# The second attention's scores: three precision passes in the rows of one matmul per head, in place of three 480-column matmuls against a block-diagonal key tile

## The reference, cut to what matters

```python
# layer 1: query = layernorm(x), kv_source = ctx_1024 (8 sequences x 120 keys x 512)
q = (query @ w_q.T).reshape(B, T_q, 16, 32)          # 16 heads of 32 features
k = (kv_source @ w_k.T).reshape(B, T_kv, 16, 32)
v = (kv_source @ w_v.T).reshape(B, T_kv, 16, 32)
attn = softmax(einsum('bqhd,bkhd->bhqk', q, k) * 32 ** -0.5)
x = x + einsum('bhqk,bkhd->bqhd', attn, v).reshape(B, T_q, 512) @ w_o.T
```

## Time and profile before

| | |
|---|---|
| median of 3 runs | 1472.74 us (1472.26 to 1474.9) |
| the profiled execution | 1471.78 us |
| its span | 1469.7 us |
| PE busy | 1321.1 us, 90% |
| DVE busy | 852.8 us, 58% |
| ACT busy | 670.9 us, 46% |
| POOL busy | 576.5 us, 39% |

### The profile page before, as it was taken

The page is one execution under the profiler, slowest core; times in us unless marked ns, Lnnn a source line. Parts: engine busy times, 40 slices in busy tenths (PEclk is TensorE's granted clock), DMA queues, the critical chain, the costliest instruction groups (busy, mean ns, idle before and its releaser), DMA issues. The chain is left out here.

```text
span 1469.7 us, 27325 instructions
## 1 busy us (share of the span) xinstructions
PE 1321.1 (90%) x10010; PEld 797.8 (54%) x10010; DVE 852.8 (58%) x1726; ACT 670.9 (46%) x1890; POOL 576.5 (39%) x755
## 2 busy tenths in 40 slices
PE   6996666758999999999959999999999999899995
PEld 3544444436777777777634444444444444476663
DVE  5566999957888888887746655122221213354450
ACT  3332666628777777777723521111111112255552
POOL 1002688843354554545220004777700200145624
PEclk9997999989999999999979999999999999999998
DMA  6042000020011111111146103021120600268845
GB/s 232 29 172 87 1 1 2 1 87 17 9 45 59 45 52 52 45 59 59 45 143 67 29 1 87 1 59 32 27 59 0 215 1 29 94 171 188 210 57 72
DMA packets 85140, 96.99 MB, mean 66 GB/s; under 512 B 41968, under 2 KB 51344, under 8 KB 85008
## 3 DMA queue, kind: packets, MB, share of 16 engines
q1 hardware_dynamic: 67600, 73.04, 16.3%
q0 software_dynamic: 13248, 21.15, 7.7%
q10 hardware_dynamic: 4160, 1.05, 0.3%
HBM read 56.82 MB, written 38.45 MB: 65 GB/s over the span
## 5 line engine op out<-in xcount | busy, mean ns | idle before, releaser
L1406 DVE SCALAR_TENSOR_TENSOR shared_hf<-shared_ps_u,shared_sg 128x512 f32<-128x512 f32 x64 | 44.2, 691 | 275.6 <-PE shared_ps_u L105 261.2
L1133 POOL DMA_INDIRECT lists<-shared_load,shared_index x128 | 126.8, 991 | 167.6 <-DVE shared_sk L1274 126.3
L105 PE MATMUL shared_ps_g<-program_xs,program_wgu 128*128 128x512 f16 x768 | 178.7, 383 | 3.2 <-PEq L97 3.2
L896 ACT ACTIVATE attention_prob<-attention_ps_s,attention_nmax 128x120 f32<-128x120 f32 x512 | 177.2, 365 | 6.2 <-DVE attention_nmax L793 6.1
L1445 PE MATMUL shared_ps_y<-shared_wd,shared_hid 128*128 128x512 f16 x768 | 176.1, 379 | 2.0 <-DVE program_res L1432 2.0
L105 PE MATMUL shared_ps_u<-program_xs,program_wgu 128*128 128x512 f16 x768 | 176.7, 380 | 0.0
L1375 ACT ACTIVATE shared_sg<-shared_ps_g 128x512 f32<-128x512 f32 x64 | 38.2, 597 | 215.6 <-PE shared_ps_g L105 215.6
L1295 POOL DMA_INDIRECT program_x<-xn_rows,program_ex_slots x40 | 38.8, 969 | 243.6 <-PE experts_ps_x L1657 148.3
L105 PEld LDWEIGHTS shared_ps_g<-program_xs,program_wgu 128*128 128x128 f16 x768 | 75.6, 98 | 95.1 <-issue 6.1
L1445 PEld LDWEIGHTS shared_ps_y<-shared_wd,shared_hid 128*128 128x128 f16 x768 | 75.0, 98 | 92.8 <-DVE program_res L1432 2.4
L105 PEld LDWEIGHTS shared_ps_u<-program_xs,program_wgu 128*128 128x128 f16 x768 | 75.3, 98 | 91.3 <-issue 1.1
(11 more groups left out here) (276 smaller groups left out, 2565.4 us busy)
## 6 DMA issues: line engine op xcount, KB each, us to landing
xn_rows<-attention_g_xn SPq DMA_DIRECT2D x32, 256.0 KB, 2.3
xt_tiles<-attention_gT SPq DMA_DIRECT2D x32, 256.0 KB, 2.1
out_rows<-program_res SPq DMA_DIRECT2D x32, 256.0 KB, 2.1
program_xs<-xt_tiles SPq DMA_DIRECT2D x28, 256.0 KB, 5.0
program_x<-in_x SPq DMA_DIRECT2D x2, 3072.0 KB, 15.7
att_qr<-in_sh_guT SPq DMA_DIRECT2D x8, 512.0 KB, 4.1
program_x<-in_dyn_gT SPq DMA_DIRECT2D x8, 512.0 KB, 4.4
program_x<-in_dyn_uT SPq DMA_DIRECT2D x8, 512.0 KB, 5.5
```

Of the source, the lines that this page charges most:

```text
L105: last = pe.matmul(out, lhs(a, k), rhs(b, k), start=n == 0, stop=n == len(terms) - 1)
L896: last = act.activation(prob[:, c, h, :], ps_s[c % 2][:, h, :], ACT.Exp, bias=nmax[:, d % 2, c, h:h + 1], accum_out=rsum[:, d % 2, n:n + 1])
L1133: pool.indirect_dma_start(out=io["lists"], out_offset=bass.IndirectOffsetOnAxis(ap=index[:, t, k:k + 1], axis=0), in_=load[:, t, k, :], in ...
L1406: dve.scalar_tensor_tensor(hf[:, c % 2], ps_u[c % 2][:, :], HS / WS, sg[:, c % 2], ALU.mult, ALU.mult).then_inc(s["hf"], 1)
```

## The change

The scores are made by head, 16 matmuls of 120 columns for a tile in place of 12 of 480. The contraction runs over 96 rows: rows 0 to 31 hold the head's 32 features of the high queries against high keys, rows 32 to 63 high queries against low keys, rows 64 to 95 low queries against high keys. So the three passes are summed inside one matmul.

For this, a head's 32 rows of `qT` (which stand at rows 0, 32, 64 or 96) have to be moved to other rows. `spread` does that with 12 transfers inside SBUF: three parts times four row groups, each of 32 rows with four pieces of 256 bytes. They are issued by SP, per tile for the queries (`packed_queries`) and per sequence for the keys (`packed_keys`; pieces of 240 bytes). `g.queries` and `g.keys` have two buffers each; `g.queries` lies where `simb` and `rs` of the earlier stages lay. `g.kbd`, its memset and `block_keys` go.

The queries are made one step earlier (in step u-2, LEAD 6 in place of 5) and all that stands before them moves with them. `qT` has one buffer instead of two, so ACT's high part for a tile waits until the transfers of the tile before have landed (`q_in`).

```diff
+COPIES = 3 * HC
-def block_keys(pool, g, b, c):
...
+def spread(sp, to, parts, done):
+    for n, src in enumerate(parts):
+        for r in range(HC):
+            sp.dma_start(to[n * DH:(n + 1) * DH, r::HC, :], src[r * DH:(r + 1) * DH, :, :]).then_inc(done, 16)
+def packed_keys(sp, g, b):
+    cols = slice(b * J, (b + 1) * J)
+    hi, lo = g.k1[:, 0, :, cols], g.k1[:, 1, :, cols]
+    spread(sp, g.keys[:, b % 2], (hi, lo, hi), g.keys_in[b % 2])
+def packed_queries(sp, g, u, qT, done):
+    spread(sp, g.queries[:, u % 2], (qT[:, 0], qT[:, 0], qT[:, 1]), done[u % 2])
 # setup, SP
                 sp.dma_start(g.x[:, NT - 12:NT, :], xs[:, NT - 12:NT, :]).then_inc(x_in[1], 16)
+                sp.wait_ge(job_hi, last_job[3])
+                sp.wait_ge(job_lo, last_job[3])
+                packed_keys(sp, g, 0)
                 sp.wait_ge(job_mm, len(jobs))
 # setup, POOL
-                pool.memset(g.kbd[:, :, :, :, :], 0.0).then_inc(kbd_zero, 1)
...
-                    block_keys(pool, g, 0, c)
 # attention1
-    LEAD, LAG = 5, 9
+    LEAD, LAG = 6, 9
-        qT = m.sb("qT", [P, 2, 2, KC, P], f16)
+        qT = m.sb("qT", [P, 2, KC, P], f16)
 # SP, step(t, d)
                         sp.dma_start(raw[:, :], io["sh_guT"][bass.ds(b * P, P), :]).then_inc(w_in, 16)
+                        if b + 1 < B:
+                            need(sp, c4["s_mm"], KC * t)
+                            packed_keys(sp, g, b + 1)
                     u = t - 7
                     if live(u):
                         sp.wait_ge(lg.ok, u + 1)
                         sp.dma_start(io["xn_rows"]...)
+                    u = t + 2
+                    if live(u):
+                        sp.wait_ge(s["q_hi"], u + 1)
+                        sp.wait_ge(s["q_lo"], u + 1)
+                        need(sp, c4["s_mm"], KC * (u - 1))
+                        packed_queries(sp, g, u, qT, q_in)
+                    u = t - 7
+                    if live(u):
                         sp.wait_ge(s["g_lo"], u + 1)
                         sp.dma_start(io["xt_tiles"]...)
 # POOL, step(t, d)
-                    if live(t) and live(t + 1) and d == TB - 1:
-                        b = t // TB
-                        for c in range(KC):
-                            pool.wait_ge(c4["s_mm"], KC * t + c + 1)
-                            block_keys(pool, g, b + 1, c)
 # ACT, c == 3
-                        u, q = t + 1, (d + 1) % 2
+                        u = t + 2
                             act.wait_ge(s["q_mm"], u + 1)
-                            need(act, c4["s_mm"], KC * (u - 1))
-                            act.activation(qT[:, q, 0], ps_q[:, :, :], ACT.Copy, scale=SC1 / WS).then_inc(s["q_hi"], 1)
+                            need(act, q_in[(u - 1) % 2], 16 * COPIES * ((u - 1) // 2 + 1))
+                            act.activation(qT[:, 0], ps_q[:, :, :], ACT.Copy, scale=SC1 / WS).then_inc(s["q_hi"], 1)
 # PE
                 def scores(u, d, c):
+                    b = u // TB
                     if c == 0:
-                        pe.wait_ge(s["q_lo"], u + 1)
-                    if d == 0:
-                        pe.wait_ge(g.keys_ok, KC * HC * (u // TB) + HC * c + HC)
+                        pe.wait_ge(q_in[u % 2], 16 * COPIES * (u // 2 + 1))
+                    if c == 0 and d == 0:
+                        pe.wait_ge(g.keys_in[b % 2], 16 * COPIES * (b // 2 + 1))
                     need(pe, c4["exp"], KC * u + c - 1)
-                    matmuls(pe, ps_s[c % 2][:, :, :], lambda a, _: qT[:, d % 2, a, c, :], lambda a, _: g.kbd[:, a, c, :, :],
-                            ks=(0,)).then_inc(c4["s_mm"], 1)
+                    for h in range(HC):
+                        n = c * HC + h
+                        last = pe.matmul(ps_s[c % 2][:, h, :], g.queries[0:3 * DH, u % 2, n, :], g.keys[0:3 * DH, b % 2, n, :],
+                                         start=True, stop=True)
+                    last.then_inc(c4["s_mm"], 1)
 # PE, DVE, ACT, POOL: u = t + 1 becomes u = t + 2 for transposes of x, xT and the queries,
 # and apply, inverse_root and statistics go from t + 2, t + 3, t + 5 to t + 3, t + 4, t + 6
```

More of the change, by code:

```diff
@@ L699, in attention1 @@
         centred, xs_in = m.sem("centred"), m.sem("xs_in")
+        q_in = [m.sem(f"q_in{n}") for n in range(2)]
         rows_out = [m.sem(f"rows_out{n}") for n in range(2)]
@@ L756, in step @@
                 def step(t, d):
-                    u = t + 3
+                    u = t + 4
                     if live(u):
-                        ln.inverse_root(pool, g, u, (d + 3) % 4)
+                        ln.inverse_root(pool, g, u, d % 4)
                     u, q = t - 6, (d + 2) % 4
@@ L842, in step @@
                         lg.statistics(dve, g, t - 4, d, waits=False)
-                    if live(t + 2):
-                        ln.apply(dve, g, t + 2, (d + 2) % 4, s["xt_mm"])
+                    if live(t + 3):
+                        ln.apply(dve, g, t + 3, (d + 3) % 4, s["xt_mm"])
                     if live(t):
@@ L849, in step @@
                         prob_low(t - 1, 2)
-                    if live(t + 5) or live(t + 4):
-                        ln.before(dve, t + 5)
+                    if live(t + 6) or live(t + 5):
+                        ln.before(dve, t + 6)
                     u, q = t - 2, d % 2
@@ L855, in step @@
                         dve.tensor_tensor(oT[:, q, 1], ps_x[:, :, :], oT[:, q, 0], ALU.subtract).then_inc(s["o_lo"], 1)
-                    if live(t + 5) or live(t + 4):
-                        ln.statistics(dve, g, t + 5, (d + 1) % 4, waits=False)
+                    if live(t + 6) or live(t + 5):
+                        ln.statistics(dve, g, t + 6, (d + 2) % 4, waits=False)
                     if live(t):
                         maximum(t, d, 3)
-                    u, q = t + 1, (d + 1) % 2
+                    u = t + 2
                     if live(u):
                         dve.wait_ge(s["q_hi"], u + 1)
-                        dve.scalar_tensor_tensor(qT[:, q, 1], ps_q[:, :, :], SC1 / WS, qT[:, q, 0], ALU.mult,
+                        dve.scalar_tensor_tensor(qT[:, 1], ps_q[:, :, :], SC1 / WS, qT[:, 0], ALU.mult,
                                                  ALU.subtract).then_inc(s["q_lo"], 1)
@@ L921, in step @@
                             exps(t, d, c)
[L922 removed]
+                        u, q = t + 2, d % 2
                         if c == 0 and live(u):
@@ L927, in step @@
                     if isinstance(t, int) and t == NT + 1:
-                        act.wait_ge(g.keys_ok, B * KC * HC)
+                        for n in range(2):
+                            act.wait_ge(g.keys_in[n], 16 * COPIES * B // 2)
                         tokens(act, g, io, 0, 0, xs_in)
@@ L1007, in step @@
                         outputs(t - 2, 3)
-                    u = t + 1
+                    u = t + 2
                     if live(u):
@@ L1039, in step @@
                         need(pe, s["q_lo"], u)
-                        queries(u, d + 1, (0, 1))
+                        queries(u, d, (0, 1))
                     if live(t - 1):
@@ L1051, in step @@
                         pe.wait_ge(s["of"], u + 1)
-                        need(pe, s["xt_lo"], min(t + 2, NT) if isinstance(t, int) else t + 2)
+                        need(pe, s["xt_lo"], min(t + 3, NT))
                         need(pe, s["l_ok"], t - 7)
                         transposed(ps_x, of).then_inc(s["o_tr"], 1)
-                    u = t + 1
+                    u = t + 2
                     if live(u):
-                        queries(u, d + 1, (2, 3)).then_inc(s["q_mm"], 1)
+                        queries(u, d, (2, 3)).then_inc(s["q_mm"], 1)
                     if not past(t, 2):
@@ L1708, in program @@
         g.x_in = [m.sem(f"x_in{n}") for n in range(3)]
-        g.keys_ok = m.sem("keys_ok")
+        g.keys_in = [m.sem(f"keys_in{n}") for n in range(2)]
         io = dict(io, out=out)
@@ L1720, in program @@
             g.qr = a.sb("qr", [P, KC, D], bf16)
-            g.rs = a.sb("rs", [P, D])
-            g.kbd = a.sb("kbd", [P, 2, KC, HC, J], f16)
+            g.keys = a.sb("keys", [P, 2, HEADS, J], f16)
+            g.queries = a.sb("queries", [P, 2, HEADS, P], f16)
+            place = g.queries[:, :, :, :].rearrange("p s h n -> p (s h n)").bitcast(f32)
+            g.simb, g.rs = place[:, 0:JB], place[:, JB:JB + D]
             setup(nc, g, io)
```

17 lines of the change are left out of this document (5 added, 12 removed).

## The result

The change made the kernel slower: 1501.84 us (median of 4 runs, 1501.41 to 1503.04) against 1472.54; the ratio is 1.020, 95% interval 1.018 to 1.021. The forecast was 1445 (range 1434 to 1470), with 13% on slower. The profiled execution took 1503.04 us, its span is 1501.2.

The account below looks back on a forecast made before the run. PE was taken as the bound, DVE close behind. Steps 2 to 29 save 33.0 us, steps 30 and 31 3.2, less 7.2 for the start and 1.5 allowance: 27.5 less, 1445 us (range 1434 to 1470).

Parts of the forecast that it names:

- Part 1, the matmuls: Score matmuls on PE: a group of four takes 0.21 us in place of 0.61, 1.60 us less per step.
- The rival of the weight loads: Weight loads set the score matmuls' pace: PE saves only 0.7 to 0.9 us per step, about 1467 us; chance 0.06.
- Part 2, what PE keeps: Ordinary step: 11.96 us, 1.18 shorter than 13.14; a quarter of PE's saving goes back to waits for DVE.
- the two waits: PE in a step: the wait for x_new grows from 0.39 to 0.52 us; a new 0.28 for xT before the logits.
- Little room: Rival: DVE or ACT give less room, the step stays above 12.5 us, total 1462 us; chance 0.10.
- Part 3, the transfers: SP's packs: 12 issues of 0.45 us plus 2.1 landing, 7.5 us per pack, hidden in the middle of the stage.
- The slack of 2.6 us: Ordinary step: the pack lands at about +7.0, ACT's next high queries come at +9.6, so no cost.
- 1.5 us of allowance: Cost allowed for seven sequence steps together, where SP also issues the keys and the pack starts some 0.7 us late.
- sequence steps collide: Rival: the double pack costs 2 us each, not 0.2, and landing is 3 us: 1457 us; chance 0.13.
- The loop's rival: The pack's loop, 4.3 + 12p (p: us per issue), sets the step: 1545 us at 0.9, 1485 at 0.75; chance 0.13.
- Part 4, the start: Stage start, where nothing hides the pack: step 2 starts 7.2 us later, with the bounds' ends 6 to 16.
- Part 5, the end: Last steps: step 30 without queries gains 2.2 us, step 31 about 1.0; removed memset, copies and setup keys worth nothing.

Follow-up runs that it names:

- e4: Changed kernel with only the high*high part of the queries packed, 4 transfers per tile in place of 12, two low passes left out: 1444.14 us, 0.9809.
- p1: Changed kernel with 72 more transfers on SP in idle layer 0, series of 12 of one kind, to price an issue: 1505.98 us in one run.
- e2: Changed kernel with the heads in another order in both packed tiles, so a row's four pieces stand side by side at the destination: 1500.37 us, 1.0187.
- e8: Packed scores of the changed kernel, moved through device memory: one store and three loads per tile, keys arranged once in setup: 1450.5 us, 0.9851.
- e3: Changed kernel with two buffers for qT, so ACT's high queries wait for the pack of two tiles before: 1486.85 us, 1.0093.

## Why the prediction was wrong, point by point

**Part 1, the matmuls: right.** 0.21 to 0.22 us per group; loads of 96 rows and 128 columns hide. The rival of the weight loads did not occur. The Trainium skill (TensorE: Matmul & The Clock Gate, "LDWEIGHTS (loading the stationary operand)") gives the length of one load; here each load of the scores is 96 ns long, near that rule, but four pairs of load and matmul pass in 0.22 us, so the loads overlap and do not set the pace.

**Part 2, what PE keeps: right.** The step is 11.94 us (forecast 11.96), with the two waits in the places and at the times worked out. It holds in eight steps of the changed kernel and, from step 8 to step 26, in all of e4 but step 9. "Little room" did not occur.

**Part 3, the transfers: this step failed.** "I take 0.45, since the later ones stand behind 256 KB each, these behind 32 KB." The price is 0.60 per issue, with what lies between 0.65 in the keys' pack (7.80 / 12) and 0.70 in the queries' (8.43 / 12). Issues 0.65 apart were a sign of being wrong by the prediction itself. p1 shows why the rows misled: none was of a transfer inside SBUF. Rows and pieces as far as p1 and e2 varied them (32 to 128 rows, one or four pieces) change little; whether both ends are in SBUF does. That is no full account of an issue's price: with one end in device memory, e8's load of the keys, 96 rows of 16 pieces, took 0.55. Landing was right (1.9, forecast 2.1). The "27 x 0.45 = 12.1 us, just over the step; starts some 0.7 late" became 18.1 us from 505.40 to 523.49 (the two packs, two stores and one load) and a start 6.0 late. The slack of 2.6 us was gone, and 1.5 us of allowance stood for 46.

The upper bound of the issue, 0.68, was in the text and close to the truth. What failed besides the choice is that only the ordinary step was worked out at both ends (pack 7.0 and 13.2). Put into the queue of the sequence's first step it gives 27 x 0.68 = 18.4 us, so a pack over 6 us late against a slack of 2.6. The rival "sequence steps collide" named this very place, but was priced at 2 us for each, where the changed kernel shows 6.8 to 9.3 for a pair. Its point of decision was not worked out: 27p passes one step of 12 us by the slack of 2.6 at p of about 0.54 us per issue. The loop's rival was priced for every step (over 0.64 by 4.3 + 12p); at 0.70 ordinary steps are still 11.94. Its 2.2 us for both parts was too long (ACT's part starts at 537.26, SP's pack at 539.14, so 1.9), and landing counts from the start of the last issue, which the sum held twice: 1.9 + 7.8 + 1.9 is 11.6, just inside the step.

Two terms were missing behind that: that a late pack costs twice, for the scores and, through the single `qT`, for ACT and the exponentials queued behind it (e3 takes that wait away: 9.5 us in the six pairs, 5.6 at the start); and that PE's clock drops after such a stand (0.69 in the stretch shown). How much of a pair is the clock alone no run here separates; in step 14 the product by itself loses 1.28 us to it.

**Part 4, the start: the mechanism right, the size not.** Step 0 came at 333.50 (forecast 331.5), step 1 at 344.94 (340.6), step 2 at 361.94 (351.9). Of the 10.0 us of miss at step 2, 2.0 are there at step 0 and 5.7 arise between steps 1 and 2, where the third pack stands behind the first keys' pack: the same price of an issue. The end given, "6 to 16", was just passed: 17.2.

**Part 5, the end: right for step 30** (10.97, 2.1 less; forecast 2.2). Behind the start of step 31 only 0.2 us were gained, where 1.0 was forecast. The keys of sequence 0 in `setup` cost nothing visible, as said.

So one number was too low (0.45 for 0.65 to 0.70), in a queue that was already full, and turned 27 us of gain into 29 of loss. With most of the query pack out of the way (e4) the time is 1444.14, beside the forecast 1445.

## What to carry to other kernels

Before an instruction stream takes over moves, add up the issues of its fullest step, not of the mean one, at the upper bound of the price, and compare that with the slack of what stands behind them. If the price is not in the trace for this kind of transfer, it is the number to measure first; here 12 transfers in an idle stretch would have told it. Few large transfers through device memory can beat many small ones inside SBUF although each byte travels twice (here by 51 us), when the sequencer's time per issue, not the bytes, is the bound.

## What the runs showed of the hardware that was not expected

In p1 an issue on SP behind another of its kind took 0.59 to 0.60 us when source and destination were both in SBUF (32 or 128 rows), 0.42 to 0.45 when one was in device memory (32, 96 or 128 rows). A store to device memory straight behind a transfer inside SBUF took 0.59, too. POOL issued the keys' transfers in 0.55. Landing inside SBUF, counted from the start of the issue, took 1.8 to 1.9 us (medians, 10 to 40 KB), hardly less than the 2.0 of a 256 KB store to device memory in e8.

An operation of DVE that reads and writes SBUF (the norm's 128x512 TENSOR_SCALAR) took 2.04 instead of 0.52 us beside a 2.14-us product of POOL. It began inside POOL's operation and ended 0.28 behind it, in each of the five sequences of e8 where they met. The Trainium skill (SBUF — State Buffer, "SBUF: two separate sides") says that the port pair that VectorE and GpSimd share is locked for a whole instruction and the other engine stands, for VectorE operations of certain kinds (in a two-port mode, or with two inputs in SBUF). The trace agrees with such a lock in its times; of which kind this operation is, no row shows.
